# Attention output normalised by way of DRAM with channels on partitions, in place of PE transposes

## The reference

```python
h = x @ W1 + b1                       # q, k, v of 16 heads, 8 channels each
w = softmax((q @ k.T) / 8**0.5, causal)
a = (w @ v) over the heads            # [512, 128]
x = layernorm(x + a @ Wp + bp)
xp = x shifted down by one token
xr, xk = mu_r*x + (1-mu_r)*xp, mu_k*x + (1-mu_k)*xp
x = layernorm(x + sigmoid(xr @ W_r.T) * (relu(xk @ W_k.T)**2 @ W_v.T))
```

## Time and profile before

| | |
|---|---|
| median of 3 runs | 726.02 us (722.94 to 727.3) |
| the profiled execution | 729.24 us, of which the span is 727.5 us |
| PE busy | 612.0 us, 84% of the span |
| DVE busy | 553.3 us, 76% |
| ACT busy | 470.4 us, 65% |
| POOL busy | 368.2 us, 51% |
| DMA | 65.80 MB, mean 90 GB/s |

### The profile page before, as it was taken

How to read it: one execution, slowest core, us unless ns; L and a number is a source line. 1 busy time by engine, 2 the same in 40 slices (tenths; PEclk the granted TensorE clock), 3 DMA queues, 4 the chain that set the end, 5 groups by cost and what they waited for, 6 DMA issues and landing times.

```text
span 727.5 us, 17681 instructions
## 1 busy us (share of the span) xinstructions
PE 612.0 (84%) x6729; PEld 275.7 (38%) x6729; DVE 553.3 (76%) x1654; ACT 470.4 (65%) x917; POOL 368.2 (51%) x518
## 2 busy tenths in 40 slices
PE   4468887898989989898989889898989898897873
PEld 2122333344343435343443434343443434342342
DVE  1476785779888787979788887979797887875327
ACT  2104773776868676777868676767768686767741
POOL 3002333455555556555646555565545565555643
PEclk9999997999999999999999999999999999999976
DMA  4752525142443636242634535342525435300011
GB/s 142 112 133 45 148 46 161 25 139 50 104 119 61 161 61 163 51 140 44 158 56 89 134 61 160 62 145 59 143 41 119 105 66 142 61 18 17 17 30 30
DMA packets 72203, 65.80 MB, mean 90 GB/s; under 512 B 9333, under 2 KB 63926, under 8 KB 72118
## 3 DMA queue, kind: packets, MB, share of 16 engines
q1 hardware_dynamic: 71410, 64.41, 37.5%
q10 hardware_dynamic: 708, 0.26, 0.2%
HBM read 34.70 MB, written 29.88 MB: 89 GB/s over the span
## 4 chain that ended last, share of the span: by engine, by line
PE 55%; DVE 20%; ACT 8%; issue 7%; POOL 4%; DMA 4%; ACTq 1%; SPq 1%; POOLq 0%; DVEq 0%
PE ops L623 15%; DVE rowmax L851 12%; PE sps L596 10%; PE tps L558 9%; PE spare L482 7%; ACT probs L764 6%; PE spare L502 4%; PE sps L581 3%; DVE h L902 3%; POOL probs L1029 2%; DMA xres<-L_attn_x 2%; PE spare L534 2%; PE spare L518 1%; DVE y L890 1%; PE spare L497 1%
## 5 line engine op out<-in xcount | busy, mean ns | idle before, releaser
L851 DVE TENSOR_REDUCE rowmax<-sps 128x1 f32<-128x512 f32 (+7 forms) x1024 | 401.3, 448 | 100.1 <-PE sps L596 99.4
L764 ACT ACTIVATE probs<-tps 128x512 f32<-128x512 f32 x640 | 346.4, 595 | 147.9 <-PE tps L558 147.9
L1029 POOL TENSOR_SCALAR_AFFINE_SELECT probs<-probs 128x512 f32<-128x512 f32 x256 | 158.8, 638 | 259.5 <-ACT probs L764 259.4
L623 PE MATMUL ops<-probs,vop 128*32 128x384 f32 (+3 forms) x2048 | 174.8, 449 | 7.1 <-POOL probs L1029 5.8
L558 PE MATMUL tps<-qop,kop 50*128 50x384 bf16 (+3 forms) x1024 | 126.9, 306 | 40.2 <-ACT probs L764 36.4
L596 PE MATMUL sps<-kop,qop 48*64 48x512 bf16 (+7 forms) x2048 | 130.4, 310 | 7.3 <-DMA kop<-d_parts 7.3
L581 PE MATMUL sps<-qmask,dup 64*128 64x128 bf16 (+1 forms) x640 | 69.7, 214 | 33.3 <-DVE rowmax L851 29.0
L558 PEld LDWEIGHTS tps<-qop,kop 50*128 50x128 bf16 x1024 | 34.2, 94 | 161.7 <-ACT probs L764 115.1
L623 PEld LDWEIGHTS ops<-probs,vop 128*32 128x32 f32 x2048 | 50.9, 110 | 82.2 <-issue 62.2
L596 PEld LDWEIGHTS sps<-kop,qop 48*64 48x64 bf16 x2048 | 43.1, 106 | 49.5 <-issue 19.3
L581 PEld LDWEIGHTS sps<-qmask,dup 64*128 64x128 bf16 x640 | 31.4, 95 | 75.6 <-DVE rowmax L851 69.3
(11 more groups left out here) (123 smaller groups left out, 585.0 us busy)
## 6 DMA issues: line engine op xcount, KB each, us to landing
qop<-d_parts SPq DMA_DIRECT2D x64, 192.0 KB, 4.3
kop<-d_parts SPq DMA_DIRECT2D x63, 192.0 KB, 4.8
d_parts<-qk_parts SPq DMA_DIRECT2D x15, 768.0 KB, 3.7
d_parts<-qk_parts SPq DMA_DIRECT2D x15, 512.0 KB, 4.9
d_parts<-qk_parts SPq DMA_DIRECT2D x17, 256.0 KB, 5.5
xa<-L_attn_x SPq DMA_DIRECT2D x16, 256.0 KB, 3.0
xres<-L_attn_x SPq DMA_DIRECT2D x16, 256.0 KB, 3.3
out<-result SPq DMA_DIRECT2D x15, 256.0 KB, 2.7
```

The source lines that it names most:

```text
L623: last = nc.tensor.matmul(ops[32 * t:32 * t + 32, BLK * a:SEQ], vop[:, par, a, QUARTET * half + t, hh, :], probs[:, g % 2, i, off:off + w] ...
L764: nc.scalar.activation(probs[:, g % 2, i, :], tps[:, bank(n), :], ACT.Exp, scale=SCALE)\
L851: last = nc.vector.reduce_max(rowmax[:, par, QUARTET * half + i, a:a + 1], sps[:, bank(n), off:off + w], axis=AX_X)
L1029: last = nc.gpsimd.affine_select(out=v, in_=v, compare_op=ALU.is_ge, fill=0.0, base=0, pattern=[[0, QUARTET], [1, BLK]], channel_multiplie ...
```

## The change

For all batches but the last (`TRANSPOSED` = 15) the uses `sums0`, `sums1` and `attnT` are gone from PE, DVE and ACT. `osum` of each half is written to DRAM (`d_o`); once that has landed, the sums come back as 128 x 32 (`sums`) and the numerators with channels on partitions (`numer`). DVE inverts the sums (`invert_sums`, end of group 2), SP writes them to `d_inv` and reads them back repeated over the eight channels of each head (`inv_rows`), and DVE multiplies (`divide`, end of group 4) straight into `attnT`. `vop` has its ones in other columns, so ACT fills it with one copy in place of two. The scaling by mu moves from ACT to POOL (groups 0 and 1). The load of `xres` moves to the front of the step. `project` waits for `attn_done`.

```diff
@@ def spare_order():
-                                      if (use, before(stage, frame)) not in FINISHED]
+                                      if (use, before(stage, frame)) not in FINISHED
+                                      and not (use in ("sums0", "sums1", "attnT")
+                                               and before(stage, frame) < TRANSPOSED)]
@@ sync
+            def move_o(n, half):
+
+                wait(sp, o_copied, 2 * n + half + 1)
+                sp.dma_start(d_o[half].rearrange("h s d n -> (h s d) n"), osum[:, half, :]).then_inc(o_out[half], 16)
+                wait(sp, o_out[half], 16 * (n + 1))
+                wait(sp, attn_done, n)
+                wait(sp, sums_inverted, n)
+                sp.dma_start(sums[:, half, :], d_o[half, :, 1, 0].rearrange("h (c n) -> h c n", n=SHARE))\
+                    .then_inc(sums_in[half], 16)
+                sp.dma_start(numer[E // 2 * half:E // 2 * half + E // 2, :],
+                             d_o[half, :, 0]).then_inc(numer_in[half], 16)
...
+                if active("D", b):
+                    wait(sp, xbias_done, n)
+                    sp.dma_start(xres[:], x[n].rearrange("(t p) e -> p t e", p=P)).then_inc(xres_in, 16)
...
+                if norm:
+                    move_o(n, 1)
                 if active("T", b):
                     load_max(par, 1, 2 * before("T", b) + 1)
...
+                if norm:
+                    wait(sp, sums_inverted, n + 1)
+                    sp.dma_start(d_inv.rearrange("f h (c n) -> (h c) f n", n=SHARE), inv_sums[:]).then_inc(inv_out, 16)
...
+                if norm:
+                    wait(sp, inv_out, 16 * (n + 1))
+                    sp.dma_start(inv_rows[:], d_inv.rearrange("f h n -> (f h) n").unsqueeze(1)
+                                 .to_broadcast([HEADS, DH, SEQ])).then_inc(inv_in, 16)
...
+                if active("T", b) and before("T", b) < TRANSPOSED:
+                    move_o(before("T", b), 0)
@@ tensor
                 elif use == "project":
-                    is_read(pe, "attnT", n, k)
+                    wait(pe, attn_done, n + 1)
@@ scalar
             def copy_o(n, half):
-                is_written(act, ("sums0", "sums1")[half], n - 1)
+                wait(act, o_out[half], 16 * n)
...
-                    if tg == 9 and active("D", tb) and before("D", tb) < LAST:
-                        scale_steps(before("D", tb))
@@ vector
+            def invert_sums(n):
+                for half in range(2):
+                    wait(dve, sums_in[half], 16 * (n + 1))
+                wait(dve, inv_out, 16 * n)
+                nc.vector.reciprocal(inv_sums[:], sums[:]).then_inc(sums_inverted, 1)
+
+            def divide(n):
+                for half in range(2):
+                    wait(dve, numer_in[half], 16 * (n + 1))
+                wait(dve, inv_in, 16 * (n + 1))
+                is_written(dve, "project", n - 1)
+                nc.vector.tensor_tensor(attnT[:], numer[:], inv_rows[:], ALU.mult).then_inc(attn_done, 1)
...
+                    if tg in (2, 4) and active("D", tb) and before("D", tb) < TRANSPOSED:
+                        (invert_sums if tg == 2 else divide)(before("D", tb))
@@ gpsimd
-            def mix_sum(n):
...
+            def mix_sum(n, i):
+                wait(pool, step_done if i == 1 else mixed_done, n + 1 if i == 1 else 2 * n + 1)
+                nc.gpsimd.tensor_scalar(scaled[:], step_d[:], mus[:, i:i + 1], None, ALU.mult).then_inc(scaled_done, 1)
+                wait(pool, scaled_done, 2 * n + 2 - i)
+                nc.gpsimd.tensor_tensor(mixed[:, i, :], scaled[:], hT[:, 0:SEQ], ALU.add).then_inc(mixed_done, 1)
```

More of the change, by code:

```diff
@@ L46 @@
 MROWS = 2
+SHARE = PAIRS * SEQ // P
 PARTS = 3
@@ L225, in block_program @@
         attn = sb("attn", [P, TT, HEADS, DH])
+        sums = sb("sums", [P, 2, SHARE])
+        inv_sums = sb("inv_sums", [P, 2, SHARE])
+        inv_rows = sb("inv_rows", [E, SEQ])
+        numer = sb("numer", [E, SEQ])
         attnT = sb("attnT", [E, SEQ])
@@ L265, in block_program @@
         biases_in = sem("biases_in")
+        d_o = nc.dram_tensor("d_o", (2, PAIRS, 2, DH, SEQ), F32, kind="Internal").ap()
+        d_inv = nc.dram_tensor("d_inv", (2, PAIRS, SEQ), F32, kind="Internal").ap()
         weights_in = sem("weights_in")
+        o_out = [sem("o_out0"), sem("o_out1")]
+        numer_in = [sem("numer_in0"), sem("numer_in1")]
+        sums_in = [sem("sums_in0"), sem("sums_in1")]
+        sums_inverted = sem("sums_inverted")
+        inv_out = sem("inv_out")
+        inv_in = sem("inv_in")
+        attn_done = sem("attn_done")
         ones_ready = sem("ones_ready")
@@ L326, in is_written @@
         def is_written(eng, use, n, taken=None):
-            if 0 <= n < BATCH and spare_bank(use, n) != taken:
+            if (use, n) in COUNTS and spare_bank(use, n) != taken:
                 eng.wait_ge(spare_written[spare_bank(use, n)], COUNTS[use, n] + 1)
         def is_read(eng, use, n, taken=None):
-            if 0 <= n < BATCH and spare_bank(use, n) != taken:
+            if (use, n) in COUNTS and spare_bank(use, n) != taken:
                 eng.wait_ge(spare_read[spare_bank(use, n)], COUNTS[use, n] + 1)
@@ L432, in step @@
                 elif active("A", b):
-                    n = before("A", b)
-                    wait(sp, qk_split, 2 * (n + 1))
-                    wait(sp, ops_in[0], LOADED * n)
+                    wait(sp, qk_split, 2 * (before("A", b) + 1))
+                    wait(sp, ops_in[0], LOADED * before("A", b))
                     wait(sp, ops_in[1], LOADED * before("S", b))
@@ L439, in step @@
                                      parts_apart(w)).then_inc(parts_out, 16)
-                    wait(sp, parts_out, 48 * n)
+                if norm:
+                    wait(sp, inv_out, 16 * (n + 1))
+                    sp.dma_start(inv_rows[:], d_inv.rearrange("f h n -> (f h) n").unsqueeze(1)
+                                 .to_broadcast([HEADS, DH, SEQ])).then_inc(inv_in, 16)
+                if active("A", b) and before("A", b) > 0:
+                    wait(sp, parts_out, 48 * before("A", b))
                     if active("T", b):
@@ L730, in spare_use @@
                     wait(act, pv_done, GROUPS * (n - 1))
-                    for hh in range(2):
-                        ins = nc.scalar.copy(vop[:, par, :, :, hh, DH * hh:DH * hh + DH],
-                                             spare[:].rearrange("k (t p h d) -> k h t p d", t=TT, p=PAIRS, h=2)[:, hh])
+                    places = vop[:, par].rearrange("k t p h (c d) -> k (t p) (h c) d", d=DH)
+                    ins = nc.scalar.copy(places[:, :, 0:7:6, :],
+                                         spare[:].rearrange("k (a h d) -> k a h d", h=2, d=DH))
                 elif use == "attnT":
+                    act.wait_ge(attn_done, TRANSPOSED)
+                    is_written(act, "project", TRANSPOSED - 1)
                     ins = nc.scalar.copy(attnT[:], spare[:])
@@ L774, in split_middle @@
                 nc.scalar.copy(part(i, 1), qk_rest[:, i, :]).then_inc(qk_middle, 1)
[L776 to L781, removed]
             def step(b):
@@ L879, in spare_use @@
                     is_written(dve, "attnT", n - 1, k)
-                    tiles = spare[:].rearrange("q (t r s h d) -> q s t r h d", t=TT, r=QUARTET, s=2, h=2)
+                    tiles = spare[:].rearrange("q (t r h s d) -> q s t r h d", t=TT, r=QUARTET, s=2, h=2)
                     nc.vector.reciprocal(inv[:, half], tiles[:, 1, :, :, :, 0]).then_inc(inv_done, 1)
-                    wait(dve, inv_done, 2 * n + half + 1)
+                    wait(dve, inv_done, half + 1)
                     for t in range(TT):
@@ L1067, in step @@
                     tb, tg = late(b, g)
-                    if tg == 0 and active("E", tb) and before("E", tb) < LAST:
-                        mix_sum(before("E", tb))
+                    if tg in (0, 1) and active("E", tb) and before("E", tb) < LAST:
+                        mix_sum(before("E", tb), 1 - tg)
                     if tg == 3 and active("E", tb) and before("E", tb) < LAST:
```

17 lines of the change are left out of this document (7 added, 10 removed).

## The result

The changed kernel takes 792.65 us (median of 4 runs, 789.6 to 796.01) against 726.11 us before (4 runs, 722.94 to 727.3): a ratio of 1.0925, interval 1.0866 to 1.0984. The predicted 738 us had the sign and the kind of loss, and missed the size by 54.6 us: the measured time lies above the stated 714 to 759, and above the 755 to 775 of the last rival too. One execution further down (e8) took 2547 us beside 699 to 708 in the three others of its kernel; it counts as disturbed and is left out.

What follows compares the result with a forecast made beforehand. PE was taken to bound a steady step's first half, DVE its second. Twelve steady steps +2.6 us, the others -4.2, clock drops +13.8 on 729.24 gave 741.4 us executed, 738 as median; range 714 to 759.

Steps and rivals of the forecast that it cites:

- the last rival: Clock drops in every step, or half 1's stores land late and delay row maxima and parts: 755 to 775 us, chance 0.12.
- 0.5 to 1 was foretold: Sign in the profile after: `inv_rows` lands 0.5 to 1 us behind the parts.
- PE stands still for 2.35 us on average (1.65 in good steps, 3.4 in bad): PE's wait ahead of `project` in a steady step: `project` can start 7.8 us after the parts' issue, PE ready after 5.45.
- The parts are issued at 399.64 ..., a time set by POOL's third part and so not moved: SP's queue: what PE sheds in groups 2 and 3 leaves the parts' issue unmoved; `inv_rows` follows at 401.6.
- slower still: Same as the last rival: 755 to 775 us, chance 0.12; its late-stores case has DVE waiting in group 2 too.
- The gain of group 0 moves the issue of the parts itself, 0.4 earlier: Group 0: without the scaling on ACT, exp starts 0.6 us earlier, 0.4 kept, so the parts go out 0.4 earlier.
- six drops ... and take 2.3: PE's clock behind the waits at `project`: six drops, each between 1.4 and 4.05 us, taken at 2.3: +14 us.
- the sum: Total of the terms: -1.6 us for the steps and +13.8 for the clock, 741.4 us executed, 738 as median.
- The steps that are not steady: Step 0: -0.6, step 1: -1, step 14: -2.1, step 15: -0.5; together -4.2 us.
- a sign of being wrong: DVE waiting at `invert_sums`, end of group 2, would show the prediction wrong; it was taken as free by 0.5 to 1 us.
- The rule of the Trainium skill: By it `inv_rows`, issued at 401.6, lands at 404.2, before PE is at `project`, and the whole saving stands.

Runs made afterwards that it cites:

- e8: e5 with the scaling by mu moved back from POOL to ACT: 706.09 us (3 runs), ratio 0.9688 to the kernel before.
- e6: The changed kernel with only the store of `d_inv` issued early, the `inv_rows` load left behind the parts: 780.78 us.
- e5: The changed kernel with the `d_inv` store ahead of SP's wait for the row maxima's store, and the `inv_rows` load ahead of `xa` and the parts: 702.9 us.
- e3: The kernel before with only the scaling by mu on POOL and the new `vop` layout with one copy of v: 730.38 us, ratio 1.0058.
- e4: The changed kernel with 12 extra matmuls on PE ahead of `project`'s wait, their results unused: 770.99 us.
- e7: The changed kernel with the `inv_rows` load issued by ACT at the end of group 4 instead of by SP: 787.99 us.

## Why the prediction was right in kind and short in size

- **Right: the kind of loss.** `project` waits for DVE's product, DVE for the DMA of `inv_rows`, in 15 of 15 batches; the clock stands at 0.50 behind it; PE's busy time rises though matmuls are gone; the landing is about 1 us behind the parts' (0.5 to 1 was foretold). `invert_sums` hardly waited in the steady steps: DVE stood idle ahead of it in three of the twelve, for 0.2, 0.2 and 0.6 us. `divide` took 0.69 for 0.7, `d_o` landed after 2.7 us as taken, the reciprocal took 0.54 within 0.35 to 0.7.
- **Wrong in size: "PE stands still for 2.35 us on average (1.65 in good steps, 3.4 in bad)".** The waits of PE in the twelve steps after the first are 3.3 to 5.9 us with a mean of 4.66. In the step shown the parts go out 15.84 us after the step's start, where I had them 0.4 earlier than the 14.94 of before: 1.3 us missed. From their issue to DVE's product it is 7.99 us (7.7 in the mean of the twelve), where I had 7.05: 0.9 missed. Twelve times 2.3 us is 28 us.
- **The step that failed is "The parts are issued at 399.64 ..., a time set by POOL's third part and so not moved".** In the kernel before SP issued the parts 0.03 us after POOL's third part in most steps, so the premise held there. In the changed kernel SP comes to them 0.0 to 2.6 us after it, 1.5 in the mean of the twelve steady steps; in the step shown it was ready at 427.65 and the parts went out at 428.49. SP had stood at the store of half 1 (landing 2.7 us), issued two loads, then the row maxima, whose 16 KB now land after 2.7 us in place of 1.4 before behind those loads, then four loads, `xa`, and `d_inv`. I priced each new transfer by the time at which its own data was needed. I didn't price what each of SP's waits and issues (0.3 to 0.6 us apiece) does to the next entry of the same fixed order. The late parts cost time only because `inv_rows` stands behind them: e6 halves their lateness to 0.8 us and PE's mean wait falls from 4.66 to 4.0 us, while in e5 they are later still and nothing is lost. Of the rival "slower still" just this half happened: row maxima and parts out late, while DVE hardly waited in group 2. It got 0.12.
- **Wrong: "The gain of group 0 moves the issue of the parts itself, 0.4 earlier".** The gap for ACT closed and one for the row maxima opened (`q` matmuls 2.45 us after the step's start against 2.36). e3 shows the same by itself: 7.4 us less waiting for ACT in all, no shorter time. The 0.4 us is part of the 1.3 above.
- **Wrong in size: "six drops ... and take 2.3".** `project` took 2.04 or 2.05 us in 14 of 15 steps; only behind the shortest wait, 1.43 us, did it run at full speed (1.13). e4 gives 21.7 us, at least, for the 13.8 in the sum: the miss here is 8 us and more. What was wrong is the number of drops, 14 for 6; the price of one lies between 1.5 and 2.4 us by e4, and the 2.3 taken is not shown to be wrong.
- **The steps that are not steady** were to give back 4.2 us. Up to the first `project` nothing is gained: the stall at `xbias` (3.78 us) gave way to one of 5.87 us at `project`. In steps 14 and 15 `project` waits 1.43 and 3.09 us, and with the end they are 9.1 us longer than before. SP stood at the row maxima's round trip ahead of `d_inv` there too (2.6 us each time). The sum had this wait in none of its steps. DVE also stood idle for 1.6 and 9.3 us ahead of `invert_sums` in these two. That was named as a sign of being wrong; the profile names no releaser, but the only waits there are for transfers. It is no new loss by itself, for e5 has the same idle times (2.4 and 8.2 us).

With the measured terms a steady step comes to -1.74 (the three uses gone) + 4.66 (the wait) + 1.5 (the clock) = +4.4 us, and to 5.3 with 2.4 for the clock; by the starts of `project` it is 4.8, between the two. Of the 54.6 us missed, 41 lie in the twelve steady steps (57.6 measured, 16.4 in the sum with its clock) and 13 in the others (9.2 against -4.2).

The rule of the Trainium skill that I set against the sum ("DMA: Bandwidth & Descriptors", section "Anatomy of one DMA": 2.0 us and the bytes at 436 GB/s) would have 256 KB land after an estimated 2.6 us. The section gives that fit for one DMA issued by GpSimd, and these are issued by SP, so it was a loose comparison from the start. A store of 256 KB takes 2.7 us; `inv_rows` takes 5.3 us with the parts ahead and 3.4 with the parts behind it (e5). The measurements decide, and neither of the last two fits the rule.

## What to carry to other kernels

Before a calculation on chip is turned into a chain of transfers, write down the whole order of issue, with each wait that the issuing engine stands at, and carry every delay through to the next entries: the same four hops came out 23 us ahead of the kernel before in one order (702.9 us) and 67 behind it in another (792.65), with the same instructions. A short transfer that the bound engine waits for belongs ahead of the large ones that nobody needs yet; another queue didn't get it past them here (e7). A wait of 4 us on PE costs its length and a stretch at half clock behind it, which matmuls that compute nothing can partly buy back (21.7 us here), though removing the wait is worth four times that.

## What the runs showed of the hardware that was not expected

- A transfer issued from ACT's own queue behind 1.5 MB issued by SP landed after 5.5 us, the same as behind them on SP's queue (5.3), against 3.4 ahead of them.
- The store of the row maxima, 16 KB, landed after 1.4 us before and in e3, and after 2.7 or 2.8 us in every kernel in which the loads of `sums` and `numer` were issued in the two microseconds ahead of it, e5 too. Which of the two loads does it was not tried.
- A multiplication by a value per partition took 1569 ns for 128 x 512 on POOL, more than an addition of two tensors of that size (1271 ns). In e3 it took 1575, so the new transfers are not the reason.
- DVE and POOL slowed each other when their operations overlapped. The four operations of `result` take 1.11 us together before and in e3, and 1.63 us in nearly every step of the kernels with the new transfers; the median of one stays at 334 to 339 ns, so it is one of the four that grows. In the changed kernel `result` starts 0.26 us into POOL's `step_d`:

```profile
411.03 1.04 POOL L1107 TENSOR_TENSOR step_d<-hT 128x512 f32<-128x512 f32 x1
```
```profile
411.29 1.63 DVE L951 TENSOR_SCALAR result<-z,moments,rstd 128x128 f32<-128x128 f32 x4
```

In e3 it starts when `step_d` has 0.1 us left:

```profile
419.16 1.04 POOL L1048 TENSOR_TENSOR step_d<-hT 128x512 f32<-128x512 f32 x1
```
```profile
420.07 1.11 DVE L894 TENSOR_SCALAR result<-z,moments,rstd 128x128 f32<-128x128 f32 x4
```

DVE's product shows the same. It takes 0.69 us in all 15 batches of the changed kernel, where no POOL operation runs beside it, and 0.83 to 1.75 us in e5, where one always does. The longest ends 0.56 us after POOL's addition:

```profile
581.36 1.26 POOL L1148 TENSOR_TENSOR z<-gated,h 128x512 f32<-128x512 f32 x1
```
```profile
581.43 1.75 DVE L950 TENSOR_TENSOR attnT<-numer,inv_rows 128x512 f32<-128x512 f32 x1 [0.28 <-DMA inv_rows<-d_inv]
```

Where the product is under way as that addition starts, POOL takes 1.70 us for it and not 1.26. The order of events in the traces speaks for POOL's work and not for the transfers; no run changes the overlap alone.
